# Attention with transposed scores, the masked one's mask added by a bf16 identity product, in a fused convolution, attention and FFN kernel

## The reference

```python
x = x + conv51(group_norm(x), weight_comp, kpe)       # depthwise, 51 x 51
t = to_tokens(x)                                       # [16, 256, 32]
t = t + masked_attention(ln(t), Wq, bq, Wk, bk, Wv, bv, Wo, bo, Ws, bs)
t = t + steps(ln(t), ffn_w1, ..., wq, wk, wv, wo, attn_mask, ffn_mask)
x = from_tokens(t, x)

def masked_attention(x):
    spikes = any image's leaky integrator over x @ Ws + bs fires at this token
    mask = (local | j % 16 == 0 | j < 4) & spikes[None, :]
    scores = where(mask, (Q @ K.T) / sqrt(32), -inf)
    return nan_to_num(softmax(scores)) @ V @ Wo + bo   # a row without a key gives 0

def step(h, p):                                        # 33 steps
    op = argmax(h[0, 0, :19])
    if attn_mask[op]: h = softmax((h@wq[op]) @ (h@wk[op]).T / sqrt(32)) @ (h@wv[op]) @ wo[op]
    if ffn_mask[op]:  h = relu(h @ w1[op] + b1[op]) @ w2[op] + b2[op]
```

## Time and profile before

| | us |
|---|---|
| median of 3 runs | 200.5 (199.66 to 201.96) |
| span of the profiled execution | 199.1 |
| convolution and layer norm, until about | 40 |
| masked attention, first exponential | 62.0 |
| last group normalised | 99.9 |
| second attention with its FFN, until the next bdv | 112.1 to 153.8 |
| third attention with its FFN | 153.8 to 194.9 |
| store of the result, until | 199.1 |

### The profile page before, as it was taken

One profiled execution on the slowest core, in us unless ns is written; L12 is line 12 of the kernel. 1 busy time (PEld: TensorE's weight loads), 2 busy tenths in 40 slices (PEclk: granted clock), 3 DMA queues, 4 the chain that ended last, 5 costly groups with the idle time before them and its releaser, 6 DMA issues.

```text
span 199.1 us, 4262 instructions
## 1 busy us (share of the span) xinstructions
PE 166.5 (84%) x1255; PEld 112.6 (57%) x1256; DVE 134.3 (67%) x382; ACT 111.3 (56%) x324; POOL 64.1 (32%) x153
## 2 busy tenths in 40 slices
PE   7999989693898998879929679999867699998770
PEld 5779744241685776647412468776533587775320
DVE  1364578819938889896506388898756689789481
ACT  3464511429767656555405568675655877664670
POOL 8940000100061555453600005655510036556300
PEclk9999999969579999999966999999999999999997
DMA  5900000000000000000000100000000000000003
GB/s 158 315 3 0 3 0 3 0 3 2 0 2 0 2 0 3 0 0 18 3 7 2 20 0 0 0 0 0 0 0 15 0 0 0 0 0 0 0 0 110
DMA packets 3020, 3.33 MB, mean 17 GB/s; under 512 B 889, under 2 KB 2361, under 8 KB 3002
## 3 DMA queue, kind: packets, MB, share of 16 engines
q1 hardware_dynamic: 2858, 2.85, 4.8%
q10 hardware_dynamic: 144, 0.25, 0.4%
HBM read 2.58 MB, written 0.53 MB: 16 GB/s over the span
## 4 chain that ended last, share of the span: by engine, by line
PE 60%; DVE 16%; issue 9%; ACT 8%; POOL 2%; DVEq 1%; ACTq 1%; POOLq 0%
PE bank L555 17%; PE bank L528 8%; PE bank L615 5%; PE bank L542 5%; ACT qz L981 4%; PE bank L679 4%; PE bank L813 3%; PE bank L512 3%; DVE big L1269 3%; PE bank L633 3%; PE bank L600 2%; POOL prob L448 2%; PE bank L694 2%; ACT qz L1050 1%; ACT prob L905 1%
## 5 line engine op out<-in xcount | busy, mean ns | idle before, releaser
L448 POOL TENSOR_SCALAR prob<-prob,einv 128x256 f32<-128x256 f32 x96 | 44.7, 478 | 60.6 <-DVE einv L1264 60.4
L1269 DVE COPY big<-bank 128x512 f32<-128x512 f32 x48 | 32.9, 685 | 5.7 <-PE bank L528 5.7
L905 ACT ACTIVATE prob<-bank,nmax 128x256 f32<-128x256 f32 x64 | 29.8, 473 | 11.6 <-DVE nmax L1256 11.6
L528 PE MATMUL bank<-ident,prob 128*128 128x128 f32 x192 | 30.2, 280 | 6.5 <-POOL prob L448 6.4
L555 PE MATMUL bank<-hT,qz 128*128 128x256 f32 x128 | 32.7, 383 | 0.0
L528 PEld LDWEIGHTS bank<-ident,prob 128*128 128x128 f32 x192 | 21.4, 140 | 18.2 <-POOL prob L448 14.1
L1256 DVE TENSOR_REDUCE nmax<-bank 128x2 f32<-128x512 f32 x32 | 21.6, 687 | 4.8 <-PE bank L555 4.6
L555 PEld LDWEIGHTS bank<-hT,qz 128*128 128x128 f32 x128 | 22.3, 190 | 3.6 <-issue 1.6
L905 ACT ACTIVATE prob<-minus,nmax 128x256 f32<-128x256 f32 x32 | 16.0, 500 | 8.9 <-DVE nmax L1253 7.9
L555 PE MATMUL bank<-kt,qz 128*128 128x256 f32 x64 | 16.5, 386 | 0.9 <-ACT prob L905 0.9
L905 ACT ACTIVATION_READ_ACCUMULATOR prob<-bank,nmax 128x1 f32 x64 | 12.9, 202 | 0.0
(11 more groups left out here) (173 smaller groups left out, 256.8 us busy)
## 6 DMA issues: line engine op xcount, KB each, us to landing
xrev<-xrev_dram SPq DMA_DIRECT2D x1, 512.0 KB, 4.5
xin<-xtok_dram SPq DMA_DIRECT2D x1, 512.0 KB, 5.0
out_dram<-outT SPq DMA_DIRECT2D x2, 256.0 KB, 3.3
maskc<-maskc_dram SPq DMA_DIRECT2D x1, 256.0 KB, 4.8
kx<-kx_dram ACTq DMA_DIRECT2D x1, 248.0 KB, 3.1
wx<-wx_dram SPq DMA_DIRECT2D x1, 216.0 KB, 2.9
constf<-constf_dram SPq DMA_DIRECT2D x1, 186.0 KB, 4.6
wa<-wa_dram SPq DMA_DIRECT2D x3, 56.0 KB, 1.8
```

Source lines behind the costliest of these rows:

```text
L448: last = nc.gpsimd.tensor_scalar(prob[b % NPB][:, ih, :], prob[b % NPB][:, ih, :], einv[:, b, ih:ih + 1], 1.0, ALU.mult, ALU.mult)
L528: mm = pe.transpose(bank[2 + b % 2][:, jh * S + ih * P:jh * S + (ih + 1) * P], prob[b % NPB][:, ih, jh * P:(jh + 1) * P], ident)
L905: e = nc.scalar.activation(prob[b % NPB][:, ih, :], scores, ACT.Exp, bias=nmax[:, b, ih:ih + 1], scale=-1.0 if masked else 1.0, accum_out= ...
L1269: nc.vector.tensor_copy(flat(probT[b % NTB]), bank[2 + b % 2][:, :]).then_inc(s_PT, 1)
```

## The change

**Scores twice.** Queries lie dense in `qT` [128, 4, 256] (four ScalarE copies instead of 16), and a product uses only the 32 rows of its image, on its row strip. PE makes the scores of each image as before (row i, column j), only for the row maxima, and again transposed (row j, column i) for the exponentials. So no transposes of probabilities, no copies of them, no multiplication by POOL: ScalarE's exponential writes `probT` itself, one instruction of 512 columns.

**The maximum's way.** The maxima have to be subtracted along columns now. POOL splits two images' maxima into three bf16 parts (five small operations in the masked part, which first floors them, four otherwise); PE turns them (`max_rows_pe`), ScalarE copies them to `mrow`, and `shift_pe` adds them to the bank by a product with ones.

**The sum's way.** POOL adds both halves of `probT` for the first 12 images (`halves`); in `weigh_pe` PE sums them with a product with ones, beside the values product in the same bank; VectorE takes the reciprocal of [128, 256] and multiplies (`normed_output`). In the masked part a product of 1e-30 is added against rows without a key.

**The mask.** `negm` and a transposed `negmT` (another 256 KB load, `maskt`) are bf16. `mask_pe` adds `negm` to the first scores by a product with a bf16 identity; `shift_pe` does so with `negmT` to the transposed ones. VectorE's masked maximum is then the plain reduction.

**Order.** PE works in pairs of images with a lag of three pairs. The loop over steps has the block of kind 1 first, then, in the same turn of the loop, kinds 2 and 3. Kind 3 makes the outputs of groups 0 and 1 before the hidden layer of groups 2 and 3. ScalarE loads the Exp table once ahead of the loop. All values products and residual drains go to VectorE and POOL, all projection drains to ScalarE; the ring of banks for tasks has two banks, and value products one of their own.

```diff
...
+        RING = 2
+        NPAIR = B // 2
+        LAG = 3
+        FIRST = 2 * LAG
+        SBANK = [b if b < FIRST else b % 3 for b in range(B)]
+        TBANKS = [3 + b % 3 for b in range(B)]
+        YBANK, MBANK = 6, 7
...
-        ATTY = "AAAA"
+        ATTY = "DDDD"
         RESY = "DDDD"
-        CENTREB = (1, 4, 5, 6)
+        CENTREB = (1, 4, 7, 6)
         VARB = (0, 2, 5, 3)
-        LPRE = "ADAD" + "ADAD"
+        LPRE = "AAAA" + "AAAA"
...
+        def attention_pool(pool, base, masked):
+            for n in range(NPAIR + 2):
+                if n < NPAIR:
+                    bs = slice(2 * n, 2 * n + 2)
+                    top2 = nmax[:, bs, :].rearrange("p b h -> p h b")
+                    rest2 = rest[:, bs, :].rearrange("p b h -> p h b")
+                    wait(pool, s_nm, base, 2 * n + 2)
+                    if masked:
+                        floored = nmin[:, bs, :].rearrange("p b h -> p h b")
+                        nc.gpsimd.tensor_scalar(floored, top2, -FLOOR, None, ALU.min).then_inc(s_floor, 2)
+                        wait(pool, s_floor, base, 2 * n + 2)
+                        top2 = floored
+                    nc.gpsimd.tensor_copy(parts[:, :, bs, 0], top2).then_inc(s_hi, 2)
+                    wait(pool, s_hi, base, 2 * n + 2)
+                    nc.gpsimd.tensor_tensor(rest2, top2, parts[:, :, bs, 0], ALU.subtract)
+                    nc.gpsimd.tensor_tensor(parts[:, :, bs, 1], top2, parts[:, :, bs, 0], ALU.subtract).then_inc(s_mid, 2)
+                    wait(pool, s_mid, base, 2 * n + 2)
+                    nc.gpsimd.tensor_tensor(parts[:, :, bs, 2], rest2, parts[:, :, bs, 1], ALU.subtract).then_inc(s_part, 2)
+                if n >= LAG + 1:
+                    for b in (2 * (n - LAG - 1), 2 * (n - LAG - 1) + 1):
+                        if b < B - GB:
+                            wait(pool, s_P, base, b + 1)
+                            nc.gpsimd.tensor_tensor(halves[:, b, :], probT[b][:, 0, :], probT[b][:, 1, :],
+                                                    ALU.add).then_inc(s_ps, 1 if b < B - GB - 1 else 1 + GB)
...
+        def mask_pe(pe, b):
+            pe.matmul(bank[SBANK[b]][:, :], identb[:, :], flat(negm[:, :, :]), start=False, stop=True).then_inc(s_S, 1)
+        def score_pe(pe, b, h, keys):
+            g, rows, at_row = strip(b)
+            mm = pe.matmul(bank[SBANK[b]][:, h * S:(h + 1) * S], qT[rows, g, h * P:(h + 1) * P], keys[rows, g, :],
+                           start=(keys is not kt or h == 0), stop=keys is not kt, tile_position=at_row)
+            if keys is not kt and h == NH - 1:
+                mm.then_inc(s_S, 1)
+        def shifted_pe(pe, b, h, keys):
+            g, rows, at_row = strip(b)
+            mm = pe.matmul(bank[TBANKS[b]][:, h * S:(h + 1) * S], keys[rows, g, h * P:(h + 1) * P], qT[rows, g, :],
+                           start=False, stop=(h == NH - 1), tile_position=at_row)
+            if h == NH - 1:
+                mm.then_inc(s_T, 1)
+        def max_rows_pe(pe, base, n):
+            wait(pe, s_part, base, 2 * n + 2)
+            to = slice(2 * C * (n % 2), 2 * C * (n % 2 + 1))
+            if n >= 2:
+                wait(pe, s_mr, base, 2 * n - 2)
+            for h in range(NH):
+                mm = pe.matmul(bank[MBANK][to, h * P:(h + 1) * P], flat(parts[:, h, 2 * n:2 * n + 2, :]), identb[:, :],
+                               start=True, stop=True, tile_position=(0, 2 * C * (n % 2)))
+            mm.then_inc(s_M, 2)
+        def shift_pe(pe, base, n, masked):
+            wait(pe, s_mr, base, 2 * n + 2)
+            for b in (2 * n, 2 * n + 1):
+                if b >= FIRST - 3:
+                    wait(pe, s_P, base, b - 2)
+                else:
+                    wait(pe, s_nm, base, b + 4)
+                g, rows, at_row = strip(b)
+                if masked:
+                    pe.matmul(bank[TBANKS[b]][:, :], identb[:, :], flat(negmT[:, :, :]), start=True, stop=False)
+                pe.matmul(bank[TBANKS[b]][:, :].rearrange("p (h s) -> p h s", h=NH), onesq[rows, :], rep(mrow[rows, g, :], NH),
+                          start=not masked, stop=False, tile_position=at_row)
         def weigh_pe(pe, base, t, k0, g):
...
+            t.drained(pe, k0 + g)
+            if t is st and g == 0:
+                pe.wait_ge(s_vb, NG * NH)
+            wait(pe, s_P, base, GB * (g + 1))
+            out = bank[YBANK]
             for jh in range(NH):
                 for q in range(GB):
                     b = g * GB + q
...
+                    pe.matmul(out[q * C:(q + 1) * C, 0:S], v[:, jh, b, :], probT[b][:, jh, :],
+                              start=(jh == 0), stop=(jh == NH - 1), tile_position=(0, q * C))
+            if t is st:
+                pe.matmul(out[:, S:2 * S], onesq[0:1, :], tiny[:, :], start=True, stop=False)
+            if g < NG - 1:
+                wait(pe, s_ps, base, GB * (g + 1) if g < NG - 2 else B)
+                for q in range(GB):
+                    mm = pe.matmul(out[q * C:(q + 1) * C, S:2 * S], onesc[:, :], halves[:, g * GB + q, :],
+                                   start=t is not st, stop=True, tile_position=(0, q * C))
+            else:
+                for jh in range(NH):
+                    for q in range(GB):
+                        mm = pe.matmul(out[q * C:(q + 1) * C, S:2 * S], onesc[:, :], probT[g * GB + q][:, jh, :],
+                                       start=t is not st and jh == 0, stop=(jh == NH - 1), tile_position=(0, q * C))
             mm.then_inc(s_task, 1)
...
+        def attention_pe(pe, base, t, k0, keys, ahead, masked=None):
+            ahead()
+            t.drained(pe, k0)
+            max_rows_pe(pe, base, 0)
+            for n in range(LAG, NPAIR + LAG):
+                if n - LAG + 1 < NPAIR:
+                    max_rows_pe(pe, base, n - LAG + 1)
+                shift_pe(pe, base, n - LAG, masked)
+                if n < NPAIR:
+                    wait(pe, s_nm, base, 2 * n - 1 if n > LAG else 2)
                 for h in range(NH):
...
+                    for i in range(2):
+                        if n < NPAIR:
+                            score_pe(pe, 2 * n + i, h, keys)
+                    for i in range(2):
+                        shifted_pe(pe, 2 * (n - LAG) + i, h, keys)
+                if masked and n < NPAIR:
+                    for i in range(2):
+                        mask_pe(pe, 2 * n + i)
+                if n >= LAG + 2 and n % 2 == 1 and n < NPAIR + LAG - 1:
+                    weigh_pe(pe, base, t, k0, (n - LAG - 2) // 2)
+                if masked and n == NPAIR + 1:
...
+            def before_spikes():
+                first_scores_pe(pe, (0, 1, 2, 3), kt)
+                pe.wait_ge(s_spk, 1)
+                st.fill_wait(pe, K_CNT)
+                pe.matmul(st.bank(K_CNT)[:, 0:S], onesb[:, :], spk[:, :], start=True, stop=True)
+                for h in range(NH):
+                    mm = pe.matmul(st.bank(K_CNT)[:, S + h:S + h + 1], spk[:, h * P:(h + 1) * P], onesb[:, 0:1], start=True, stop=True)
+                mm.then_inc(s_task, 1)
+                for h in range(NH):
+                    transposed_pe(pe, K_RES + h, tok, h)
+                spare(bank[5], 6)
+                first_scores_pe(pe, (4, 5), kt)
+                pe.wait_ge(s_idb, 1)
+                pe.wait_ge(s_negm, 1)
+                for b in range(FIRST):
+                    mask_pe(pe, b)
+                pe.wait_ge(s_negmT, NH)
...
+            attention_pe(pe, 0, st, K_ATT, kt, before_spikes, first_token0)
...
+            def copy_rows(n):
+                wait(act, s_M, base, 2 * n + 2)
+                to = slice(2 * C * (n % 2), 2 * C * (n % 2 + 1))
+                nc.scalar.activation(mrow[to, n // 2, :], bank[MBANK][to, 0:S], ACT.Copy).then_inc(s_mr, 2)
+            copy_rows(0)
+            for n in range(NPAIR):
+                if n + 1 < NPAIR:
+                    copy_rows(n + 1)
+                for b in (2 * n, 2 * n + 1):
+                    wait(act, s_T, base, b + 1)
+                    nc.scalar.activation(flat(probT[b]), bank[TBANKS[b]][:, :], ACT.Exp).then_inc(s_P, 1)
...
+            def normed_output(t, k, g, to):
+                t.filled(dve, k)
+                link(nc.vector.reciprocal(sinv[:, g, :], bank[YBANK][:, S:2 * S]))
+                return nc.vector.tensor_tensor(to[:, g, :], bank[YBANK][:, 0:S], sinv[:, g, :], ALU.mult)
...
+            def attention_dve(base, masked, output, late=None):
+                for b in range(B):
                     row_max(base, b, masked)
...
+                    if b == B - 3:
+                        output(0)
+                    if late and b >= B - 2 - GB and b < B - 2:
+                        late(b - (B - 2 - GB))
+                output(1)
...
```

More of the change, by code:

```diff
@@ new lines, in _ @@
+                with pe.If(kind == 1):
+                    t = Tasks(FF, pe.snap(reg_task), pe.snap(reg_da), pe.snap(reg_dd))
+                    pe.wait_ge(s_hlo, 2)
```

(37 more changed lines are left out.)

551 lines of the change are left out of this document (233 added, 318 removed).

## The result

The changed kernel takes 246.1 us (median of 4 runs, 245.4 to 248.6), the kernel before 201.1 on the same chip; the ratio is 1.227 with a 95% interval of 1.217 to 1.236. The forecast was 216, with a range to 229: the sign was right and the size was not. It is 30 us too low, and the result lies 17 above the range.

What follows compares the result with a forecast made beforehand. PE, busy 84% of the span, was taken as the bound. Span 199.1 + 14.7 (masked attention) - 5.3 (first FFN) + 2.7 + 3.2 (later attentions with FFN) = 214.4; 1.4 more gives 215.8, rounded up to 216; 8-in-10 range 203 to 229.

Steps and rivals of the forecast that it cites:

- Theory W: Experiments' theory: the time is PE's wait at the sums, 17.8 us over six times, and the half clock each brings.
- new wait: At the first and second values step of each attention PE waits about 2.8 us for POOL's sums of halves, six times.
- First masked exponential: Start of the masked attention's exponentials: forecast at 70.0 us, 8.0 later than before.
- pairs of the masked part: Masked attention: the groups of successive image pairs end 3.1 us apart.
- unmasked pairs: Unmasked attentions: a pair of images takes 2.05 us without the wait for the sums.
- last masked exponential: End of the masked attention's exponentials: forecast at 103.3 us.
- The first FFN: After the masked attention: PE takes no branch, so a 3.4 us wait and 1.9 of half-clock products go, -5.3 us.
- a fall of the clock: PE dropping to half clock in the six waits: a fall doubles some 2 us of PE work; the sum included none.
- rival (a): The clock falls in most of the six waits: 4 x 2 us, 224 us in all; chance 17%.
- Rival (c): Sums are in time and PE doesn't stand at the values steps: 198 us, faster than before; chance 10%.
- Tiling changes: On PE, each change between whole array and strips costs 0.17 us; at no cost the sum would be 9 us lower.
- rival R: Experiments' rival: products on strips are too light a load and keep the clock low whatever the wait; 229 us if reordered.

Runs made afterwards that it cites:

- the reordered kernel: The changed kernel with POOL adding the probT halves of an earlier pair ahead of the split of the current pair's maxima; 208.9 us, ratio 1.040 to the kernel before.
- before_kind1: The kernel before with only PE's loop rewritten so that the block of kind 1 stands first; 197.4 us against 201.4, ratio 0.990.
- both_twice: Changed kernel with POOL's halves ahead of its split and the first scores' mask on VectorE, plus every 128x256 reciprocal made twice; 234.6 us, ratio 1.169.
- fill_two: The changed kernel with 24 spare PE products ahead of the sums of groups 0 and 1 only, where PE waits; 227.9 us, ratio 1.145.

## Why the prediction failed, and where it held

**The plan of the work held.** Theory W is the prediction's own new wait. First masked exponential 70.2 (70.0), six waits of 17.8 us together (6 x 2.8 = 16.8), pairs of the masked part 2.9 apart at the full clock in the reordered kernel (3.1), unmasked pairs 2.0 (2.05). The last masked exponential was late by 10 us; 26 us of PE work at the half clock stand between the first and the last one, and half of them, 13, cover it.

**The first FFN held, within 0.6 us.** From the last group to bdv -4.7 us, forecast -5.3; the direct test on the kernel before gave -3.5 in the trace, 4 in the medians and 2 by the ratio.

**What failed is the price of a fall of the clock.** The sum put falls in the six waits at nothing, and their price was too low. The prediction said "A fall doubles some 2 us of PE work", and gave rival (a), "Clock falls in most of the six waits", 8 us and a chance of 17%. The falls came (at the first five waits; at the sixth the clock was still down), and the PE work done at half between one wait and the return of the clock was 6.5, 13.4, 3.4, 10.2 and 19.9 us. Half of each is its cost, so 3.2, 6.7, 1.7, 5.1 and 10.0 us where the prediction had 2. That is 53 of the 78.7, or 27 us of cost against the 8 of rival (a); 19 more stand at three other places that the forecast gave no fall: at the first masked pairs (6.8), in the normalisation (6.4) and around the start of the third attention (6.0). All in all half-clock work grew by 64.7 us, which costs 32. The sum without it, 243.5 - 32.4 = 211.1 of span, lies 3 us below the 214.4 forecast (6 below, if one counts that the forecast had already taken out the 4.7 us at the first FFN). Two errors made the price. I took the length from the one fall of the earlier trace rows that I had, where the clock came back after five us of work. And I counted each fall for itself, while here the next wait comes before, or soon after, the clock is back. "Against it that each wait is followed by five us of steady work" was no argument against: PE worked through 13 us without a pause, at half.

**The sign's rival.** Rival (c), sums in time, 198: the reordered kernel is that case, at 209. Of the 11 us that it lacks, 8 are half of the half-clock work that it has over the kernel before (30.0 against 14.0).

**Tiling changes.** The 0.17 for each was not tested alone. The pair distances that rest on it came out within 0.2 us.

**What stays open.** Which idle time lets the clock fall, and when it comes back, can't be told from these runs: a wait of 1.15 us brought no fall, those of 2.7 to 3.3 did, and in the third the fall came only 1.1 us after PE had resumed (windows of 1 us, same columns as above). Falls also stand where no sums wait, as at 69.3 and at 185.4 in the kernel after, and one long wait is not needed: in before_kind1 the clock fell at 183.6, behind 3 us in which PE was busy 0.54, 0.60 and 0.37 of each and its longest wait was 1.03 us (second group of windows). Whether products on strips delay the clock's return, as rival R could still claim, no run tests. The Trainium skill (TensorE: Matmul & The Clock Gate, Part 1: The HAM clock gate) has half speed as the default that activity lifts. That filling the waits gave 18 us agrees. That in the kernel after PE worked 13 us without a pause before the clock came back is not explained by that rule alone.

```profile
152.00:153.00 1.00, 0.00 (x0) 0.00 (x0) 0.00 (x0) 0.00 (x0) 1.00 (x3) 1.00 0.00 0
153.00:154.00 1.00, 0.48 (x8) 0.16 (x8) 0.00 (x0) 0.00 (x0) 0.47 (x1) 1.00 0.00 0
154.00:155.00 1.00, 1.00 (x16) 0.82 (x16) 0.00 (x0) 0.38 (x1) 0.00 (x0) 0.82 0.00 0
155.00:156.00 1.00, 1.00 (x14) 0.64 (x6) 0.00 (x0) 0.00 (x0) 0.00 (x0) 0.50 0.00 0
```

```profile
180.00:181.00 1.00, 0.54 (x5) 0.31 (x4) 0.47 (x1) 1.00 (x4) 0.82 (x2) 1.00 0.00 0
181.00:182.00 1.00, 0.60 (x4) 0.36 (x4) 0.75 (x3) 0.98 (x3) 0.35 (x1) 1.00 0.00 0
182.00:183.00 1.00, 0.37 (x3) 0.37 (x4) 0.33 (x1) 0.57 (x1) 0.58 (x2) 1.00 0.00 0
183.00:184.00 1.00, 1.00 (x12) 0.64 (x11) 0.67 (x1) 0.26 (x1) 0.00 (x0) 0.81 0.00 0
```

## What to carry to other kernels

Here six waits of PE of 2.4 to 3.3 us cost their length (some 18 us) and as much again for the clock behind them. So price such waits with the clock in them, look in the trace for how long a fall lasts and not for one example, and when such waits follow each other, reckon with a clock that is down for much of the way between them. Before shortening anything, look at what stands in front of the late operation on its own engine: here two additions behind a split that nobody needed yet cost 37 us. If a wait can't be moved, fill it with spare products, and only where PE does stand idle: the same 24 products at three places where it didn't cost 6 us (233.9 against 227.9).

## What the runs showed of the hardware that I had not expected

- In the kernel after, PE at 1.2 GHz for 13.6 us (96.6 to 110.3) and for 23.9 (205.8 to 229.7), with no idle moment once it had resumed in the first case and one wait of 2.38 us and a few shorter ones in the second.
- 21.0 us more of VectorE work (both_twice), with VectorE at 59%, made the kernel 30 us longer.
- Making PE do 24 more products at each of six places (fill_two) made the kernel 18 us shorter.
- A reciprocal of 128x256 on VectorE takes 1.75 us, 4.1 times a multiplication of the same size (0.42); it is 6.8 ns an element, as the two small ones in the earlier trace rows let expect (6.0).
